# Sixteen-head attention of a two-layer network: PSUM as four single score banks and three single maxima banks, where it was three and two pairs

## The reference

```python
# layer 0: causal, rotary q and k, scale sqrt(8)
scores = jnp.einsum('bhsd,bhtd->bhst', q, k) / scale
scores = jnp.where(causal[None, None], scores, -jnp.inf)
attn = jax.nn.softmax(scores.astype(jnp.float32), axis=-1).astype(x.dtype)
out = jnp.einsum('bhst,bhtd->bhsd', attn, v)
# layer 1: no mask, low-rank q, k, v, scale sqrt(16 + 64 + 64)
attn = jnp.einsum('bhqd,bhkd->bhqk', query, key) / scale
attn = jax.nn.softmax(attn, axis=-1)
out = jnp.einsum('bhqk,bhkd->bhqd', attn, value)
```

## Time and profile before

| | us |
|---|---|
| median of 3 runs | 1882.09 (1865.8 to 1890.54) |
| the profiled execution, its time | 1888.39 |
| its span | 1886.5 |
| TensorE matmul busy | 1735.7 (92%) |
| VectorE busy | 1159.0 (61%) |
| ScalarE busy | 1157.5 (61%) |
| GpSimd busy | 81.4 (4%) |
| mean granted TensorE clock | 0.894 of 2.4 GHz |

### The profile page before, as it was taken

How to read it: one execution, slowest core, us unless ns; L and a number is a source line. 1 busy time by engine, 2 the same in 40 slices (tenths; PEclk the granted TensorE clock), 3 DMA queues, 4 the chain that set the end, 5 groups by cost and what they waited for, 6 DMA issues and landing times. The chain is left out here.

```text
span 1886.5 us, 31101 instructions
## 1 busy us (share of the span) xinstructions
PE 1735.7 (92%) x12744; PEld 799.2 (42%) x12744; DVE 1159.0 (61%) x1566; ACT 1157.5 (61%) x2092; POOL 81.4 (4%) x158
## 2 busy tenths in 40 slices
PE   6889999999998999676999999999999999599999
PEld 3444433433335444332333333333333334467776
DVE  7566677788614110359898899999999852411111
ACT  3446667668784222240788888888888887133433
POOL 3110101000000000020000000000000000000000
PEclk9567788889898999775899999999999999689999
DMA  3100000000000000100000000000000000010000
GB/s 100 62 1 1 1 1 1 1 1 1 1 1 1 1 0 0 53 1 0 1 1 2 1 1 1 2 1 1 2 1 1 2 1 1 1 35 19 14 22 22
DMA packets 16763, 17.07 MB, mean 9 GB/s; under 512 B 2994, under 2 KB 13695, under 8 KB 16127
## 3 DMA queue, kind: packets, MB, share of 16 engines
q1 hardware_dynamic: 16639, 15.32, 2.6%
HBM read 14.26 MB, written 1.05 MB: 8 GB/s over the span
## 5 line engine op out<-in xcount | busy, mean ns | idle before, releaser
L559 DVE TENSOR_REDUCE maxp<-banks 128x2 f32<-128x1024 f32 (+3 forms) x800 | 943.5, 1200 | 214.1 <-PE banks L430 107.9
L539 ACT ACTIVATE probs<-banks 128x512 f32<-128x512 f32 (+3 forms) x1664 | 855.6, 571 | 242.7 <-PE banks L442 220.9
L455 PE MATMUL banks<-probs,V 128*9 128x256 f32 (+3 forms) x6272 | 508.9, 398 | 7.0 <-POOL probs L508 6.1
L442 PE MATMUL banks<-Q,K 64*128 64x512 f32 (+3 forms) x1664 | 466.3, 507 | 27.8 <-ACT Q L524 20.6
L423 PE MATMUL banks<-K,Q 64*128 64x512 f32 (+3 forms) x1664 | 394.3, 453 | 28.8 <-DVE maxp L559 27.9
L442 PEld LDWEIGHTS banks<-Q,K 64*128 64x128 f32 x1664 | 191.5, 194 | 411.1 <-ACT probs L539 305.4
L423 PEld LDWEIGHTS banks<-K,Q 64*128 64x128 f32 x1664 | 188.1, 210 | 81.8 <-DVE maxp L559 64.8
L455 PEld LDWEIGHTS banks<-probs,V 128*9 128x9 f32 x6272 | 93.6, 89 | 257.9 <-ACT probs L539 188.7
L951 DVE SCALAR_TENSOR_TENSOR x<-banks,wts,x 128x128 f32<-128x128 f32 x128 | 36.0, 344 | 198.1 <-PE banks L914 198.1
L939 ACT ACTIVATE work<-banks,eb 128x512 f32<-128x512 f32 x128 | 86.3, 687 | 105.2 <-PE banks L905 102.8
L914 PEld LDWEIGHTS banks<-work 128*128 128x128 f32 x1024 | 118.1, 192 | 11.5 <-issue 11.5
(11 more groups left out here) (126 smaller groups left out, 861.3 us busy)
## 6 DMA issues: line engine op xcount, KB each, us to landing
tables<-in_tables SPq DMA_DIRECT2D x2, 2048.0 KB, 9.7
work<-in_ew SPq DMA_DIRECT2D x16, 256.0 KB, 3.0
flex<-in_h SPq DMA_DIRECT2D x2, 1024.0 KB, 8.1
x<-in_x SPq DMA_DIRECT2D x4, 256.0 KB, 4.3
out<-x SPq DMA_DIRECT2D x4, 256.0 KB, 2.3
cst<-in_consts SPq DMA_DIRECT2D x1, 865.0 KB, 6.1
flex<-in_w SPq DMA_DIRECT2D x3, 256.0 KB, 3.0
flex<-in_w_qk SPq DMA_DIRECT2D x1, 256.0 KB, 5.9
```

Source lines behind the costliest of these rows:

```text
L442: mm = pe.matmul(ebank(e)[:, first:CW], k.K[rows, 2 * g + b, kt * P:(kt + 1) * P], k.Q[rows, n % 3, b, first:CW], start=True, stop=True)
L455: mm = pe.matmul(acc[32 * j:32 * j + HD + 1, low:high], k.V9[:, kt, g * HG + j, :], k.probs[:, slot + j, low:high], start=(kt == 0), stop= ...
L539: act.activation(k.probs[:, HG * (s % 2) + j, first:CW], ebank(e)[:, first:CW], ACT.Exp, scale=scale).then_inc(e_done, 1)
L559: dve.tensor_reduce(dst, src, AX.X, ALU.max).then_inc(m_done, 1)
```

## The change

The bank split becomes a table per layer, and the two halves of a maxima job may be separate jobs. With the values set, both layers have four score banks (0 to 3) and three single maxima banks (4 to 6), and each maxima job holds one half: one matmul per block, its own mask matmuls, its own wait, its own reduction from one bank. Job m waits for the reduction of job m - 3. `plan` deals out twice as many jobs with the same code and the same cost per job.

```diff
-E_BANKS = 3
+BANK_SPLIT = ((4, ((0,), (1,))), (4, ((0,), (1,))))
...
+    E_BANKS, max_halves = BANK_SPLIT[layer]
+    M_JOBS = (7 - E_BANKS) // len(max_halves[0])
...
-        out = [(t, (b,), a, CW, False) for a in range(c if causal else C) for t in range(TC) for b in (0, 1)]
+        out = [(t, (b,), halves, a, CW, False) for a in range(c if causal else C) for t in range(TC)
+               for b in (0, 1) for halves in max_halves]
         if causal:
             for t in range(TC):
-                out += [(t, heads, c, (t + 1) * P, True) for heads in (((0, 1),) if t < 2 else ((0,), (1,)))]
+                out += [(t, blocks, halves, c, (t + 1) * P, True) for blocks in (((0, 1),) if t < 2 else ((0,), (1,)))
+                        for halves in max_halves]
...
-        mpair = lambda m: k.banks[:, 3 + 2 * (m % 2):5 + 2 * (m % 2), :]
+        mbanks = lambda m: k.banks[:, E_BANKS + len(max_halves[0]) * (m % M_JOBS):
+                                   E_BANKS + len(max_halves[0]) * (m % M_JOBS + 1), :]
...
-                if m >= 2:
-                    pe.wait_ge(m_done, m - 1)
+                if m >= M_JOBS:
+                    pe.wait_ge(m_done, m - M_JOBS + 1)
                 for q, b in enumerate(blocks):
-                    for half in (0, 1):
+                    for place, half in enumerate(halves):
                         rows = slice(HALF * half, HALF * half + HALF)
-                        out = mpair(m)[:, half, q * w:(q + 1) * w]
+                        out = mbanks(m)[:, place, q * w:(q + 1) * w]
                         mm = pe.matmul(out, k.Q[rows, n % 3, b, t * P:(t + 1) * P],
                                        k.K[rows, 2 * g + b, a * CW:a * CW + w], start=True, stop=True)
                     if diagonal:
                         for hh in (0, 1):
-                            for half in (0, 1):
+                            for place, half in enumerate(halves):
...
-                if len(blocks) == 2:
-                    src = mpair(m)[:, :, 0:2 * w].rearrange("p i (b w) -> p i b w", b=2)
-                    dst = k.maxp[:, n % 2, a, t, :].rearrange("p (b i) -> p i b", i=2)
-                else:
-                    src, dst = mpair(m)[:, :, 0:w], k.maxp[:, n % 2, a, t, 2 * blocks[0]:2 * blocks[0] + 2]
+                src = mbanks(m)[:, :, 0:len(blocks) * w].rearrange("p i (b w) -> p i b w", b=len(blocks))
+                dst = k.maxp[:, n % 2, a, t, :].rearrange("p (b i) -> p i b", i=2)
+                dst = dst[:, halves[0]:halves[-1] + 1, blocks[0]:blocks[-1] + 1]
                 dve.tensor_reduce(dst, src, AX.X, ALU.max).then_inc(m_done, 1)
```

More of the change, by code:

```diff
@@ L352, in plan @@
         widths = [CW - first_col(n, kt) for kt in range(steps[n]) for _ in (0, 1)]
-        costs = [len(reductions(m)[i][1]) * (reductions(m)[i][3] + P) for m, i in todo]
+        costs = [len(reductions(m)[i][1]) * (reductions(m)[i][4] + P) for m, i in todo]
         slots, done = [], 0
@@ L412, in score_maxima @@
                 c, g = units[n]
-                t, blocks, a, w, diagonal = reductions(n)[i]
+                t, blocks, halves, a, w, diagonal = reductions(n)[i]
                 m = m_base[n] + i
@@ L426, in score_maxima @@
                         for hh in (0, 1):
-                            for half in (0, 1):
+                            for place, half in enumerate(halves):
                                 rows = slice(HALF * half, HALF * half + HALF)
                                 low = (q + 1) * w - P + HALF * hh
-                                mm = pe.matmul(mpair(m)[:, half, low:low + HALF], k.mask_max[rows, hh, :],
+                                mm = pe.matmul(mbanks(m)[:, place, low:low + HALF], k.mask_max[rows, hh, :],
                                                k.ident64[rows, :], start=False, stop=True, skip_group_check=True)
@@ L550, in reduce @@
             def reduce(n, i):
-                t, blocks, a, w, _ = reductions(n)[i]
+                t, blocks, halves, a, w, _ = reductions(n)[i]
                 m = m_base[n] + i
                 dve.wait_ge(m_ready, m + 1)
-                if len(blocks) == 2:
-                    src = mpair(m)[:, :, 0:2 * w].rearrange("p i (b w) -> p i b w", b=2)
-                    dst = k.maxp[:, n % 2, a, t, :].rearrange("p (b i) -> p i b", i=2)
-                else:
-                    src, dst = mpair(m)[:, :, 0:w], k.maxp[:, n % 2, a, t, 2 * blocks[0]:2 * blocks[0] + 2]
+                src = mbanks(m)[:, :, 0:len(blocks) * w].rearrange("p i (b w) -> p i b w", b=len(blocks))
+                dst = k.maxp[:, n % 2, a, t, :].rearrange("p (b i) -> p i b", i=2)
+                dst = dst[:, halves[0]:halves[-1] + 1, blocks[0]:blocks[-1] + 1]
                 dve.tensor_reduce(dst, src, AX.X, ALU.max).then_inc(m_done, 1)
```

## The result

The changed kernel takes 1902.73 us as the median of 20 runs (1885.99 to 1920.02), the kernel before 1881.22 (20 runs); the ratio is 1.0137 with a 95% interval of 1.0109 to 1.0165. It is slower by a little, clear of zero but under 2%. The medians differ by 21.5 us; the ratio, which is an estimate over the undisturbed runs and not the quotient of the two medians, stands for 26 us at 1880, and its interval for 20 to 31. It lies in the forecast's range of 1898 to 2005 only because that was drawn down to take in rival C.

A forecast was written before the change was run, and what follows sets the result against it. TensorE's order of work was taken as the bound. Terms 3 + 12 + 7 + 55 + 15 - 33 + 8 = +67, rounded down to +64 and added to the 1882.1 median, gave 1946 us (3.4% slower), range 1898 to 2005.

The forecast's parts named there:

- rival C: First layer's diagonal: split cells are hidden, their cost falls to about 10 us, total 1901; chance 0.15.
- (c): First layer's diagonal: split cells lose their concurrency and are paid twice, +55 us, bounds 0 and +63.
- (a): VectorE: twice as many reductions, 0.60 us pace for 512 elements; +3 us, in the second layer's prologue.
- (b): Second layer: three single maxima banks make slots late, +12 us; accumulator copy and shift operations before the ring, +7.
- (d): First layer, units 6, 7, 10, 11: uneven slots of halves +5 us, bursts at the shallow ring +10.
- (e): Unit edges, both layers: fourth score bank saves -27 us, units without maxima -6; bounds -12 and -50.
- (f): First layer's clock: longer cells at unit edges hold it low longer, +8 us, bounds -60 and +20.
- A: Second layer: VectorE becomes the bound because half reductions don't overlap, +70 us on top, 2010; chance 0.12.
- B: First layer: fourth score bank closes edge waits, so the clock stays up; 1853 us, not slower; chance 0.11.

The follow-up runs named there:

- diag_order: Kernel before, pairs and banks kept, but each half's diagonal masks issued directly behind its own matmul: 1876.66 us against 1878.03, ratio 0.9996.
- p_b34: Changed kernel with three score and four single maxima banks, halves dealt out two by two: 1892.59 us, ratio 1.0083 against the kernel before.
- b_3_4: Changed kernel with three score and four single maxima banks in both layers: 1888.00 us against 1878.03 for the kernel before, ratio 1.0071.
- c_3_3: Changed kernel with three score and three single maxima banks, one bank idle, both layers: 1937.37 us, ratio 1.0325 against the kernel before.
- p_after: Changed kernel with its banks, but the planner deals out halves two by two: 1922.51 us against 1874.67 for the kernel before, ratio 1.0256.
- l0_3_3: Kernel before, but first layer halved with three score and three single maxima banks: 1913.83 us against 1876.28, ratio 1.0196.
- l0_3_4: Kernel before, but first layer halved with three score and four single maxima banks: 1885.92 us against 1876.28, ratio 1.0060.
- l0only: First layer as changed, second layer as in the kernel before: 1889.07 us against 1876.28 for the kernel before, ratio 1.0069.

## Why the prediction was wrong

**(c) is the step that failed:** "Mask weights use the same rows as the matmul in front of them and wait until it has streamed, and matmul 1 stands behind them, so a cell is paid twice." The first half of the sentence holds, the second does not: matmul 1 uses the other rows and doesn't stand behind them. Its +55 measured 0 for the order within a cell (diag_order). For whole halves in a row, as the change has them, the halves still run side by side (p_b34, after), one cell out of step, which is worth 6 to 10 us of lag in sum; and all that halving costs the first layer is +11. The Trainium skill, "TensorE: Matmul & The Clock Gate" (Part 3, The mechanism), says that matmuls keep program order in start and end; I had drawn the full term from it. This trace disagrees across row groups (a score at 325.40 ahead of masks at 325.74), and the measurement decides. The bound of 0 was in my working; I chose near the far end although the pairs and masks of the earlier trace rows already showed the two halves side by side.

**(a) held.** 1600 reductions at a pace of 0.598, where I took 0.60; the second layer up to its first copy went from 107.4 to 109.1 us by halving (b_3_4, one profile each), where I had +3.

**(b) held in size in the second layer, but its parts were off, and it was missed in the first.** The slots alternate as I had worked out. The ring cost 1.46 per unit, 22 us in the layer, for my 19. Of the 1.46 the copy was 0.6. The steady slots are longer by 0.02 and not 0.03, which makes 0.5 for 27 of them, where I had 0.84. The rest, 0.4, is in two slots in mid-unit, 1.49 and 1.36 long in c_3_3 (from 1242.6 us), while VectorE runs the small operations for the shift (1242.2 to 1243.6); copy and small operations together are 1.0, where I had 0.5. The two errors nearly cancel.

**(d)** had +15 in all: +5 for uneven slots and +10 for bursts at the ring. In its place stand +11 for halving in the first layer and +26 for the ring there, so it is 22 short. The reasons were not the right ones either. Dealing the halves out evenly made it no better (p_b34) or worse (p_after). As far as the traces show, halving costs by the lag behind diagonal cells (up to 10 us) and by bursts that take longer as halves (15 slots at 0.23 are some 3 us). The ring costs in units 0 to 7, whereas I had priced bursts in units 6, 7, 10 and 11. In the long units it is little: at full clock 79 slots of two halves have a mean of 1.28 in l0_3_3 against 1.24 in l0_3_4, 30 of three halves 1.85 against 1.82, together 4 us. How the early units lose it is open, and part may come through the clock: c_3_3's profile has 251 us at half clock in the first layer, b_3_4's 173, but l0_3_3 and l0_3_4 only 189 and 173. One profile each does not separate waits from clock.

**(e) was right in size:** -33 predicted, -35 measured; per unit of the second layer -0.70 for the -0.8 taken.

**(f)** had +8 with wide bounds, and no run shows it. Executions of before at a granted clock of 0.905 take 1871 to 1876 us, those of after 1903 to 1906, some 30 us more at the same clock; so the loss is not one of a lower mean clock. The clock moved more between executions of one kernel (0.895 to 0.918, 34 us) than between the kernels' medians.

The account by the runs: halving +13, ring +48, fourth score bank -35, together +26. This closes by how the parts are formed; that the two layers add up, as measured apart, is the check on it. The forecast had +64. Without (c), 9 to 12 are left: (d) was then 22 too low, (f) 8 too high, and the others within a few us.

**Rivals.** C came true in mechanism: half 1's matmul slips beside half 0's masks, and of (c) about 10 is left. That its time came so near (1901 against 1903) is in part luck, as the ring in the first layer and (f) were off in opposite ways. A was wrong: halves overlap, units stayed at 43.9. (Its sum is off too: 1946 and 70 are 2016, not 2010.) B needed low stretches to vanish; in the profiled execution they shrank (121 us in the first layer against 206), but the median and l0only's clock of 0.85 show that this was that execution more than the kernel.

## What to carry to other kernels

A ring of buffers is judged by its tightest moments: in the steady slot, the time from the last read of a bank to the next matmul that needs it; beside it, every other operation that the reading engine puts in front of a release. Here one bank fewer in the maxima ring cost 48 us and one more in the score ring gave 35, so equal bank counts were not equal worth. A cost that is shown in one kind of slot need not be where the time went: lay the copies of two traces side by side and see which units grew. Before an order of instructions is priced, look in the trace whether instructions of different row groups wait for each other at all; a small reordering of the old kernel tests it, and it should have the very order of the new one.

## What was unexpected in the hardware

TensorE's two halves (rows 0 to 63 and 64 to 127) behave as two lanes: a matmul of one started 0.34 us before masks of the other that stand ahead of it in the program.

The granted clock of the same kernel varies by execution, 0.895 to 0.918, and 34 us of time with it; one profile per kernel misled by more than the effect. The lengths of units at full clock were the same from run to run within 0.03 us, and told the difference that spans hid.
